# A two-block vision tower on one core: the first norm of the second block's tokens moved into rows of tokens, and routed slots counted with a running sum

## The chip, the cores and the metric

One NeuronCore of one Trainium2 chip. The metric is device time in microseconds (us) of one execution. Engines are named as in the profile: PE is TensorE (PEld its weight loads), DVE VectorE, ACT ScalarE, POOL GpSimd, SP SyncE.

## The reference, cut to what matters

128 images of 3 x 176 x 208 become 143 patches of 16 x 16 and a class token: 144 tokens (S) of 128 features (D) each. Block 0 adds a gated state-space layer and an FFN with 8 experts, of which each token takes 2. Block 1 adds windowed attention and an FFN with one expert of 16 per image. What the change touches is the end of block 0's FFN and the norm behind it:

```python
x = _ln(mv + x, ln2_g, ln2_b)                  # x2, 128 features a token
logits = x @ gate_w + gate_b
topv, topi = jax.lax.top_k(logits, 2)
probs = jax.nn.softmax(topv, axis=-1)          # the two weights
moe = sum over the two experts of weight * expert(x)
x = _ln(moe + x, ln3_g, ln3_b)                 # called norm 3 below
h = h + x                                      # h2 in the kernel
h = h + attention(_layernorm(h))               # that norm is norm 4 below
```

All in fp32.

## The kernel before, in words

The work goes in 32 items of 4 images (T = 576 tokens). Three stages follow each other. Activations lie feature by feature (128 partitions) x token, so a norm over features is a matmul with the matrix `center` (which takes the mean away), a Square, a matmul with `mean`, and a Ln and an Exp (for the root) on full tiles of 128 x 576.

**Stage A** (lines 496 to 1046) computes block 0 up to the router. It is a pipeline by hand: in each of 35 steps four items x, y, z, w at different depths pass through, and each engine has its own `step` function, whose order of jobs is fixed (PE 557, ACT 685, DVE 825, POOL 1018, SP 367). Engines wait for each other on semaphores. Item z is routed: `turn` (534) transposes x2 into rows of tokens, 96 partitions (G) x 6 groups (NG) x 128; ACT copies them out of PSUM as `rows` (741, 750); DVE finds the two best experts (`route_...`, 934 to 1009). The place of a token in its expert's list is a rank: the tokens that chose the expert before it. `ranks` (543) forms it on PE: one matmul of `before` (ones above the diagonal) over the 96 tokens of the group, five that add each group's picks to all later groups, and one for the tokens of former items (`chosen`). Each fp32 matmul runs as two passes. POOL scatters the rows into `expert_in` by 12 indirect DMAs; SP stores h1 and x2, both feature by token, to HBM. Five table loads of ACT stand in a step (688, 702, 734, 760, 775), the one at 688 at the very beginning, though 775 has loaded the same set at the end of the step before.

**Stage B** (1053 to 1294) runs 152 blocks of 256 rows through their experts.

**Stage C** (1297 to 1961) is again a pipeline by hand, of 36 steps; in step t it holds items v = t, w = t-1, x = t-2, y = t-3, z = t-4. PSUM has banks A0, A1 for projections and others for scores. For v: SP loads h1c and x2c; DVE writes row numbers (`place`, 1829); POOL gathers 12 x 96 rows of `expert_out` (1466), multiplies them by the weights (1474) and adds the two choices to `ysum` (1479); PE transposes `ysum` to features (`moe`, 1506, 6 transposes, at the end of the step, 1705). For w: DVE adds x2c (`prec`, 1885); PE centres it (1664), ACT squares (`square`, 1716), PE takes the mean (1674), ACT Ln and Exp (`inverse_root`, 1720), DVE multiplies (`x3`, 1937) and adds bias and h1c (`h2`, 1943). Norm 4 of h2 follows (1688, 1696, 1718 to 1724, `xq` 1961). For x: attention in nine units, each a round of scores (PE 1528), `minimum` (DVE 1842), `exps` (ACT 1747), `turn` (PE 1550, a transposition), `turned` (ACT 1756), `values` (PE 1558), and `halves` and `heads` (DVE 1848 to 1861, ends in `att`). Units 6 to 8 of an item are finished in the next step, when it is y; then its projection, `h` (1911), norm 5 (`xm`, 1923, from bank A1), `means` (1932) and the routing of the image. For z: gates (`gdiag`, 1990) and last layer. Each engine takes the jobs of all items in the order of its `step` (PE 1602, ACT 1763, DVE 1877), in which a late result holds up everything behind it.

## Time and profile before

| | us |
|---|---|
| median of 3 runs | 3320.6 (3319.63 to 3323.88) |
| the profiled execution | 3318.28 |
| its span, first to last instruction | 3316.4 |
| PE busy in the span | 2775.0 |
| DVE, ACT, POOL busy | 1901.2, 1843.2, 1134.6 |
| mean granted clock of PE | 0.901 of full |

How to read it: the profile is one execution of the program on the chip, seen by the hardware's profiler. Busy time is that of instructions at work; an engine that waits is idle. The start of a matmul is measured, its end is modelled. The rows below are from the trace of this execution; times count from the first instruction.

### The profile page before, as it was taken

How to read it: one execution, taken by the hardware profiler on the slowest of the kernel's cores; microseconds unless marked ns; L12 is line 12 of the kernel's file. 1: busy time of each engine (PE TensorE's matmuls, PEld its weight loads, DVE VectorE, ACT ScalarE, POOL GpSimd, SP SyncE). 2: the span in 40 equal slices, each digit the busy share in tenths (PEclk: the TensorE clock that was granted, in tenths of full speed). 3: DMA queues.
4: the chain of work that ended last, by engine and by line, in shares of the span. 5: the costliest groups of instructions: out<-in, count | busy, mean ns of one | idle time of the engine just before them, and what ended most of it. 6: DMA issues, size and time to landing. Idle time of an engine off the chain costs nothing.

```text
span 3316.4 us, 69976 instructions
## 1 busy us (share of the span) xinstructions
PE 2775.0 (84%) x25687; PEld 2181.5 (66%) x25687; DVE 1901.2 (57%) x4527; ACT 1843.2 (56%) x3725; POOL 1134.6 (34%) x964
## 2 busy tenths in 40 slices
PE   6999999999999859999996677877788777877787
PEld 4766666666666549999995456655566555655565
DVE  4878878878788742222221355655565555655566
ACT  4777777777777734444443345544454444544454
POOL 1454555655555530000002533333333333333310
PEclk9999999999999979999998688887888888878888
DMA  3222222222222137777774111111111111111110
GB/s 119 88 84 72 96 83 72 101 78 75 100 76 73 42 114 228 228 230 227 230 228 140 34 40 41 29 41 44 44 40 27 43 44 43 40 28 44 44 30 26
DMA packets 139758, 287.14 MB, mean 87 GB/s; under 512 B 25440, under 2 KB 82784, under 8 KB 135392
## 3 DMA queue, kind: packets, MB, share of 16 engines
q1 hardware_dynamic: 114912, 245.68, 22.9%
q0 software_dynamic: 24576, 37.80, 4.2%
q8 instruction: 177, 2.90, 0.4%
q14 instruction: 93, 0.76, 0.1%
HBM read 215.08 MB, written 68.29 MB: 85 GB/s over the span
## 4 chain that ended last, share of the span: by engine, by line
PE 47%; issue 7%; another core or an unknown queue 4%; DVE 3%; ACT 1%; POOL 1%; DMA 0%; SPq 0%; DVEq 0%; ACTq 0%; POOLq 0%
PE psum L1174 8%; PE psum L1165 8%; PE psum L1538 7%; PE psum L1498 5%; PE psum L1555 3%; PE psum L1568 3%; PE psum L1523 2%; PE psum L1503 2%; PE psum L1580 2%; DVE qdiag L1837 1%; PE psum L1598 1%; PE psum L1156 1%; PE psum L1546 1%; DVE inv L1852 1%
## 5 line engine op out<-in xcount | busy, mean ns | idle before, releaser
L1466 POOL DMA_INDIRECT ycho<-expert_out,place x384 | 367.5, 957 | 1417.4 <-DVE place L1829 1309.7
L1208 ACT ACTIVATE hid<-psum,w_blk 128x256 f32<-128x256 f32 x608 | 269.1, 474 | 326.2 <-PE psum L1165 326.2
L1039 POOL DMA_INDIRECT expert_in<-rows,slot_i x384 | 392.3, 1022 | 133.2 <-issue 111.6
L1852 DVE RECIPROCAL inv<-psum 128x64 f32<-128x64 f32 x288 | 159.5, 554 | 464.7 <-remote 385.9
L1538 PE MATMUL psum<-keys,qdiag 64*64 64x80 f32 x4608 | 281.4, 256 | 124.1 <-issue 123.7
L1752 ACT ACTIVATE ex<-psum,smin 128x80 f32<-128x80 f32 x1152 | 282.2, 332 | 142.9 <-DVE smin L1845 135.8
L1538 PEld LDWEIGHTS psum<-keys,qdiag 64*64 64x64 f32 x4608 | 214.8, 148 | 211.1 <-issue 195.7
L502 PE MATMUL psum<-xn,w_in 128*128 128x288 f32 x1024 | 311.1, 429 | 39.6 <-DVE xn L861 10.2
L1174 PE MATMUL psum<-w_blk,hid 128*128 128x128 f32 x2432 | 296.6, 275 | 0.0
L1568 PE MATMUL psum<-ex_t,pair_ones 128*32 128x64 f32 x4608 | 137.8, 244 | 189.6 <-DVE half L1853 124.0
L1165 PE MATMUL psum<-x_t,w_blk 128*128 128x256 f32 x1216 | 289.5, 381 | 2.4 <-DMA w_blk<-w_exp_in 2.4
L1174 PEld LDWEIGHTS psum<-w_blk,hid 128*128 128x128 f32 x2432 | 283.7, 192 | 0.1
L1760 ACT ACTIVATE ex_t<-psum 128x512 f32<-128x512 f32 x288 | 174.1, 605 | 174.6 <-PE psum L1555 92.2
L502 PEld LDWEIGHTS psum<-xn,w_in 128*128 128x128 f32 x1024 | 187.8, 196 | 111.4 <-DVE xn L861 23.5
L1015 POOL TENSOR_TENSOR unit<-unit 128x576 f32<-128x576 f32 x64 | 119.4, 1865 | 393.7 <-ACT unit L671 276.2
L1568 PEld LDWEIGHTS psum<-ex_t,pair_ones 128*32 128x32 f32 x4608 | 86.5, 119 | 240.8 <-DVE half L1853 128.5
L1165 PEld LDWEIGHTS psum<-x_t,w_blk 128*128 128x128 f32 x1216 | 212.8, 191 | 34.4 <-DMA w_blk<-w_exp_in 2.8
L1273 DVE COPY x_t<-psum 128x256 f32<-128x256 f32 x152 | 64.6, 425 | 230.5 <-PE psum L1156 230.5
L508 PE MATMUL psum<-xin,w_tok 128*128 128x286 f32 x768 | 194.0, 409 | 2.5 <-DVEq L469 2.5
L1555 PE MATMUL psum<-cst,ex 128*128 128x128 f32 x1152 | 182.0, 280 | 7.5 <-ACT ex L1752 5.2
L1281 DVE TENSOR_TENSOR rows_out<-psum,w_blk 128x256 f32<-128x256 f32 x152 | 64.6, 425 | 215.7 <-PE psum L1174 215.7
L805 DVE SCALAR_TENSOR_TENSOR acc<-pj,taps,acc 128x576 f32<-128x576 f32 x192 | 182.3, 950 | 0.1
(247 smaller groups left out, 5848.5 us busy)
## 6 DMA issues: line engine op xcount, KB each, us to landing
w_blk<-w_exp_in SPq DMA_DIRECT2D x152, 578.0 KB, 3.8
xin<-x_in SPq DMA_DIRECT2D x32, 1716.0 KB
rows_in<-expert_in SPq DMA_DIRECT2D x152, 128.0 KB, 2.3
expert_out<-rows_out SPq DMA_DIRECT2D x152, 128.0 KB, 3.0
h_dram<-h SPq DMA_DIRECT2D x32, 288.0 KB
x_dram<-x SPq DMA_DIRECT2D x32, 288.0 KB
h1c<-h_dram SPq DMA_DIRECT2D x32, 288.0 KB
x2c<-x_dram SPq DMA_DIRECT2D x32, 288.0 KB
```

Source lines behind the costliest of these rows:

```text
L502: last = nc.tensor.matmul(bank[:, g, 0:T2], w, two(src)[:, g, :], start=True, stop=True)
L508: last = nc.tensor.matmul(bank[:, g, 0:2 * NPATCH], w_tok[:, k, :], xin[x.s][:, k, g * 2 * NPATCH:(g + 1) * 2 * NPATCH], start=(k == 0), s ...
L1039: pool.indirect_dma_start(out=expert_in[:, :], out_offset=bass.IndirectOffsetOnAxis(ap=slot_i[z.s][:, n:n + 1], axis=0), in_=rows[z.s][:, ...
L1165: nc.tensor.matmul(HB[b.s][c % HK], w_blk[b.q][:, c * 128:(c + 1) * 128], x_t[b.s][:], start=True, stop=True).then_inc(hid_done[b.s], 1)
L1174: last = nc.tensor.matmul(YB[b.s][:, t * 128:(t + 1) * 128], hid[b.s][:, c, t * 128:(t + 1) * 128], w_blk[b.q][:, FF + c * D:FF + (c + 1) ...
L1208: nc.scalar.activation(hid[b.s][:, c, :], HB[b.s][c % HK], ACT.Gelu_apprx_tanh, bias=w_blk[b.q][:, FF + FC * D + c:FF + FC * D + c + 1]).t ...
L1466: pool.indirect_dma_start(out=ycho[x.s][:, k, :], out_offset=None, in_=expert_out[:, :], in_offset=bass.IndirectOffsetOnAxis(ap=place[x.s] ...
L1538: nc.tensor.matmul(bank[at, b * QK:(b + 1) * QK], qdiag[at, u * UB + b, :, :].rearrange("p j q -> p (j q)"), keys[at, m, key_range(qb)], s ...
L1555: done = nc.tensor.transpose(XB[0:KW, b * 128:(b + 1) * 128], ex[u][:, b, :], C("ident"))
L1568: nc.tensor.matmul(sum_bank()[at], pair_ones[:, j, :], ex_t[u % RING][:, :, t * PH + j * QB:t * PH + (j + 1) * QB], start=(j == 0), stop=( ...
L1752: done = nc.scalar.activation(ex[u][:, b, in_window(qb)], score_bank(u)[:, b * QK:(b + 1) * QK], ACT.Exp, bias=smin[u % RING][:, b:b + 1], ...
L1852: v.reciprocal(inv[:], sum_bank()).then_inc(head_step, 1)
```

## The change

Stage A. `before` has 1 taken from every entry, so that it also subtracts the group's own column sum. `picks` and a new tile `upto_g` lie expert by group on the free axis; `within` is 1 except at the first group of each expert, and one scan over 48 elements (`tensor_tensor_scan`) gives in `upto_g` the picks of this and all former groups. It takes the place of the reduction `newly`. The rank is then three matmuls in place of seven, and PE waits for the scan (step 15 of the routing) instead of `picks` (step 13). `chosen` takes its sum from `upto_g`. The table load at the beginning of a step (688) is gone; one is done before the first step. x2 is stored to HBM in rows of tokens, from `rows`, once ACT has copied them; DVE no longer waits for the store two items back, ACT does before it overwrites `rows`.

Stage B. Two constants more are made before the blocks: `shift3` (the centred ln3_b) by one matmul and a copy, and ln3_b is added to `att_bias`.

Stage C. Norm 3 is done in rows of tokens ahead of the transposes. x2c is loaded as rows (96 x 768); POOL adds it to the gathered rows in a third operation. DVE takes statistics of each token (6 `bn_stats`, 6 `bn_aggr`, in two places of its order), ACT the root (a Ln and an Exp of 96 x 6), DVE the product -mean x root (`move3`), ACT writes `nrows` = ysum x root + move3 in 6 instructions of 96 x 128. PE transposes `nrows`, now in the step of w, to bank A1 where `prec` was centred; DVE makes h2 = A1 x ln3_g + h1c in one operation from PSUM. ln3_b is left out of h2 and comes back as `shift3` in norm 4 (in the Square and in `xq`) and in `att_bias`. Gone are `prec`, the two projections of norm 3, its Square, Ln and Exp, and `x3`. POOL's last sum waits for `nrows` of the item before, where it waited for the transposes.

The diff, cut to its core (indentation cut by 8; declarations, constants and semaphores left out):

```diff
@@ -124,7 +124,7 @@
 "ident": np.eye(128),
-"before": (p[:, None] < p[None, :])[:, :G],
+"before": (p[:, None] < p[None, :])[:, :G] - 1.0,
 "ones": np.ones((128, 128)),
@@ -372,8 +379,9 @@
         if z:
-            hold(sp, x2_step, z.upto(2, 2))
-            sp.dma_start(x2_dram[:, a_range(z.n, z.s)], x2[z.s][:]).then_inc(x2_stored[z.s], 16)
+            hold(sp, rows_ready, z.upto(2, 2))
+            sp.dma_start(x2_dram[row_range(z.n, z.s), :], rows[z.s][:].rearrange("p g d -> p (g d)")
+                         ).then_inc(x2_stored[z.s], 16)
@@ -542,15 +553,12 @@
-        pe.wait_ge(route_step, z.upto(ROUTE, 13))
+        pe.wait_ge(route_step, z.upto(ROUTE, 15))
         if z.old(1):
...
         dst = rank_bank(bank)
-        nc.tensor.matmul(dst, C("before")[0:G, :], picks[z.s][:], start=True, stop=False)
-        for g in range(NG - 1):
-            nc.tensor.matmul(dst[:, g + 1:NG, :], C("ones")[0:G, 0:G],
-                             picks[z.s][:, g:g + 1, :].to_broadcast([G, NG - 1 - g, E]),
-                             start=False, stop=False)
+        nc.tensor.matmul(dst, C("before")[0:G, :], by_group(picks[z.s][:]), start=True, stop=False)
+        nc.tensor.matmul(dst, C("ones")[0:G, 0:G], by_group(upto_g[z.s][:]), start=False, stop=False)
         nc.tensor.matmul(dst, C("ones")[0:G, 0:G], chosen[:].unsqueeze(1).to_broadcast([G, NG, E]),
@@ -685,7 +694,6 @@
-        act.preload_act_table_set("gelu_apprx_tanh_and_others")
         if y:
@@ -738,6 +746,7 @@
                 act.wait_ge(scattered[z.s], 16 * 2 * NG * z.n)
+                act.wait_ge(x2_stored[z.s], 16 * z.n)
             nc.scalar.activation(rows[z.s][:, 0:4, :].rearrange("p g d -> p (g d)"), A0[0:G, 0, 0:4 * 128],
@@ -863,8 +872,6 @@
             v.wait_ge(rstd3, z.upto(1, 1))
-            if z.old(2):
-                v.wait_ge(x2_stored[z.s], 16 * z.n)
             v.scalar_tensor_tensor(out=two(x2[z.s][:]), in0=both(A1), scalar=shift1[:, 0:1], in1=two(rf[:]),
@@ -966,11 +973,10 @@
     route_after(v, z, 12)
-    v.tensor_tensor(picks[s][:], pick1[s][:], pick2[s][:], ALU.add).then_inc(route_step, 1)
+    v.tensor_tensor(by_group(picks[s][:]), pick1[s][:], pick2[s][:], ALU.add).then_inc(route_step, 1)
     v.tensor_tensor(wexp[s][:], top2[s][:], top1[s][:], ALU.subtract).then_inc(route_step, 1)
     route_after(v, z, 13)
-    v.tensor_reduce(newly[s][:], picks[s][:].rearrange("p g e -> p e g"), AX_X, ALU.add
-                    ).then_inc(route_step, 1)
+    v.tensor_tensor_scan(upto_g[s][:], within[:], picks[s][:], 0.0, ALU.mult, ALU.add).then_inc(route_step, 1)
@@ -978,7 +984,7 @@
         v.wait_ge(chosen_new, z.upto(1, 0))
-    v.tensor_tensor(chosen[:], chosen[:], newly[s][:], ALU.add).then_inc(chosen_new, 1)
+    v.tensor_tensor(chosen[:], chosen[:], by_group(upto_g[s][:])[:, NG - 1, :], ALU.add).then_inc(chosen_new, 1)
     v.tensor_tensor(cand[s][:], rank_bank(bank), R("first")[0:G, :].unsqueeze(1).to_broadcast([G, NG, E]),
@@ -1423,7 +1437,10 @@
         sp.dma_start(h1c[x.s][:], h1_dram[:, a_range(x.n, x.s)]).then_inc(h_landed[x.s], 16)
-        sp.dma_start(x2c[x.s][:], x2_dram[:, a_range(x.n, x.s)]).then_inc(h_landed[x.s], 16)
+        if x.old(2):
+            hold(sp, ysum_step, x.upto(YSUM, -YSUM))
+        sp.dma_start(x2c[x.s][:].rearrange("p g d -> p (g d)"), x2_dram[row_range(x.n, x.s), :]
+                     ).then_inc(x2_landed[x.s], 16)
@@ -1473,11 +1490,13 @@
                            ).then_inc(ysum_step, 1)
-        pool.wait_ge(ysum_step, x.upto(2, 1))
+        pool.wait_ge(x2_landed[x.s], 16 * x.n + 16)
+        pool.wait_ge(ysum_step, x.upto(YSUM, 1))
+        pool.tensor_tensor(x2c[x.s][:], x2c[x.s][:], ycho[x.s][:, 0:NG, :], ALU.add).then_inc(ysum_step, 1)
+        pool.wait_ge(ysum_step, x.upto(YSUM, 2))
         if x.old(1):
-            pool.wait_ge(moe_done, x.upto(1, 0))
-        pool.tensor_tensor(ysum[:], ycho[x.s][:, 0:NG, :], ycho[x.s][:, NG:, :], ALU.add
-                           ).then_inc(ysum_step, 1)
+            pool.wait_ge(nrows_ready, x.upto(1, 0))
+        pool.tensor_tensor(ysum[:], x2c[x.s][:], ycho[x.s][:, NG:, :], ALU.add).then_inc(ysum_step, 1)
@@ -1504,9 +1523,9 @@
     def moe(x, bank):
-        pe.wait_ge(ysum_step, x.upto(2, 2))
+        pe.wait_ge(nrows_ready, x.upto(1, 1))
         for g in range(NG):
-            last = nc.tensor.transpose(bank[:, g // 3, (g % 3) * G:(g % 3 + 1) * G], ysum[:, g, :],
+            last = nc.tensor.transpose(bank[:, g // 3, (g % 3) * G:(g % 3 + 1) * G], nrows[:, g, :],
                                        C("ident")[0:G, 0:G])
@@ -1660,25 +1677,15 @@
                 pe.wait_ge(val_ready, x.upto(NV, 2))
-            pe.wait_ge(prec_ready, w.upto(1, 1))
-            project(A1, C("center"), prec[:]).then_inc(norm3_pe, 1)
+            moe(w, A1)
         if x:
...
             values(x, 2)
-        if w:
-            if y:
-                pe.wait_ge(norm5_act, y.upto(3, 2))
-            elif x:
-                pe.wait_ge(k_ready, x.upto(1, 1))
-            pe.wait_ge(norm3_act, w.upto(3, 1))
-            project(A0, C("mean"), sq3[:]).then_inc(norm3_pe, 1)
         if x:
...
         if y:
-            if w:
-                pe.wait_ge(norm3_act, w.upto(3, 2))
             router(y, A0)
@@ -1692,17 +1699,13 @@
                 pe.wait_ge(pick_step, y.upto(PICK, 1))
+            elif x:
+                pe.wait_ge(k_ready, x.upto(1, 1))
             pe.wait_ge(norm4_act, w.upto(3, 1))
...
             turn(x, 6)
-        if v:
-            if w:
-                pe.wait_ge(norm4_act, w.upto(3, 2))
-            elif v.old(1):
-                pe.wait_ge(prec_ready, v.upto(1, 0))
-            moe(v, A0)
         if x:
@@ -1713,9 +1716,24 @@
-    def square(x, dst, bank, pe_done, done):
+    def square(x, dst, bank, pe_done, done, **bias):
         act.wait_ge(pe_done, x.upto(2, 1))
-        nc.scalar.activation(two(dst[:]), both(bank), ACT.Square).then_inc(done, 1)
+        nc.scalar.activation(two(dst[:]), both(bank), ACT.Square, **bias).then_inc(done, 1)
...
+    def row_root(x):
+        act.wait_ge(stats_ready, x.upto(1, 1))
+        nc.scalar.activation(root3[:], stats[:, :, 1], ACT.Ln, bias=eps_col[0:G, 0:1]).then_inc(root_step, 1)
+        act.wait_ge(root_step, x.upto(2, 1))
+        nc.scalar.activation(root3[:], root3[:], ACT.Exp, scale=-0.5).then_inc(root_step, 1)
...
+    def normed_rows(x):
+        act.wait_ge(moved_ready, x.upto(1, 1))
+        if x.old(1):
+            act.wait_ge(moe_done, x.upto(1, 0))
+        for g in range(NG):
+            last = nc.scalar.activation(nrows[:, g, :], ysum[:, g, :], ACT.Identity, bias=move3[:, g:g + 1],
+                                        scale=root3[:, g:g + 1])
+        last.then_inc(nrows_ready, 1)
@@ -1782,29 +1800,29 @@
             exps(x, 1)
+        if w:
+            row_root(w)
+        if x:
             turned(x, 0)
...
             exps(x, 2)
+        if w:
+            normed_rows(w)
         if y:
...
             exps(x, 3)
-        if w:
-            square(w, sq3, A1, norm3_pe, norm3_act)
         if x:
...
             turned(x, 3)
-        if w:
-            inverse_root(w, r3, A0, norm3_pe, norm3_act)
-        if x:
             exps(x, 5)
...
         if w:
-            square(w, sq4, A1, norm4_pe, norm4_act)
+            square(w, sq4, A1, norm4_pe, norm4_act, bias=shift3[:, 0:1])
         if x:
@@ -1859,6 +1877,28 @@
                         one_head[:], inv[:], ALU.mult).then_inc(att_ready, 1)
...
+    def row_halves(x):
...
+        v.wait_ge(ysum_step, x.upto(YSUM, YSUM))
+        for g in range(NG):
+            last = v.bn_stats(halves3[:, g, :], ysum[:, g, :])
+        last.then_inc(halves3_ready, 1)
...
+    def row_stats(x):
+        v.wait_ge(halves3_ready, x.upto(1, 1))
+        if x.old(1):
+            v.wait_ge(moved_ready, x.upto(1, 0))
+        for g in range(NG):
+            last = v.bn_aggr(stats[:, g, :], halves3[:, g, :])
+        last.then_inc(stats_ready, 1)
...
+    def row_moves(x):
+        v.wait_ge(root_step, x.upto(2, 2))
+        if x.old(1):
+            v.wait_ge(nrows_ready, x.upto(1, 0))
+        v.scalar_tensor_tensor(out=move3[:], in0=stats[:, :, 0], scalar=-1.0, in1=root3[:], op0=ALU.mult,
+                               op1=ALU.mult).then_inc(moved_ready, 1)
@@ -1898,9 +1934,13 @@
             pick_gate(v, z)
+        if w:
+            row_halves(w)
         if y:
...
             heads(y, 8)
+        if w:
+            row_stats(w)
         if x:
@@ -1912,6 +1952,8 @@
             minimum(x, 2)
+        if w:
+            row_moves(w)
         if z:
@@ -1933,16 +1975,12 @@
         if w:
-            v.wait_ge(norm3_act, w.upto(3, 3))
-            v.scalar_tensor_tensor(out=two(x3[:]), in0=both(A1), scalar=V("ln3_g"), in1=two(r3[:]),
-                                   op0=ALU.mult, op1=ALU.mult).then_inc(x3_ready, 1)
+            v.wait_ge(moe_done, w.upto(1, 1))
+            v.wait_ge(h_landed[w.s], 16 * w.n + 16)
+            v.scalar_tensor_tensor(out=two(h2[:, w.s * T:(w.s + 1) * T]), in0=both(A1), scalar=V("ln3_g"),
+                                   in1=two(h1c[w.s][:]), op0=ALU.mult, op1=ALU.add).then_inc(h2_ready, 1)
         if x:
             halves(x, 3)
-        if w:
-            v.wait_ge(x3_ready, w.upto(1, 1))
-            v.scalar_tensor_tensor(out=h2[:, w.s * T:(w.s + 1) * T], in0=x3[:], scalar=V("ln3_b"), in1=h1c[w.s][:],
-                                   op0=ALU.add, op1=ALU.add).then_inc(h2_ready, 1)
-        if x:
             heads(x, 3)
@@ -1958,8 +1996,8 @@
                 v.wait_ge(val_done, w.upto(NV, 0))
-            v.tensor_tensor(two_two(xq[:]), both(A1).rearrange("p g (m n) -> p g m n", m=2),
-                            two(r4[:]).rearrange("p g (m n) -> p g m n", m=2), ALU.mult).then_inc(xq_ready, 1)
+            v.scalar_tensor_tensor(out=two(xq[:].rearrange("p m n -> p (m n)")), in0=both(A1), scalar=shift3[:, 0:1],
+                                   in1=two(r4[:]), op0=ALU.add, op1=ALU.mult).then_inc(xq_ready, 1)
```

## Rows read from the trace of the kernel before

**Rows 1.** The page, first part: busy time, share of span, instructions.
```profile
PE 2775.0 (84%) x25687; PEld 2181.5 (66%) x25687; DVE 1901.2 (57%) x4527; ACT 1843.2 (56%) x3725; POOL 1134.6 (34%) x964
```

**Rows 2.** Stretches: length, busy us by engine, granted clock, DMA share, GB/s.
```profile
601.36:636.30 34.94, 31.86 (x148) 23.59 (x148) 28.48 (x57) 26.54 (x38) 19.72 (x16) 1.00 0.25 85
...
2450.00:2478.00 28.00, 28.00 (x445) 21.78 (x442) 20.91 (x59) 18.01 (x52) 3.49 (x2) 0.90 0.03 7
2432.00:2450.00 18.00, 6.68 (x90) 4.90 (x91) 4.53 (x14) 3.62 (x9) 12.58 (x13) 0.68 0.31 88
3221.00:3257.00 36.00, 35.58 (x606) 27.64 (x605) 27.75 (x81) 25.65 (x71) 0.00 (x0) 1.00 0.11 32
```

**Rows 3.** Timeline, stage A: start, length, engine, work, count [idle before <-releaser].
```profile
605.39 0.24 DVE L972 TENSOR_REDUCE newly<-picks 96x8 f32<-96x48 f32 x1
...
605.46 0.34 PE L549 MATMUL psum<-picks,cst 96*96 96x48 f32 x2 [1.40 <-ACT unit L671]
...
605.63 0.98 PE L551 MATMUL psum<-picks,cst 96*96 96x40 f32 x10
...
606.65 1.20 PE L502 MATMUL psum<-xn,w_in 128*128 128x288 f32 x4
...
608.86 0.74 ACT L772 ACTIVATE rf<-psum,eps_col 128x576 f32<-128x576 f32 x1 [1.15 <-PE psum L502]
...
609.75 6.02 PE L508 MATMUL psum<-xin,w_tok 128*128 128x286 f32 x24
...
612.39 1.28 ACT L688 ACT_TABLE_LOAD   x1
...
616.77 0.74 ACT L682 ACTIVATE view<-psum,mv_bias 128x576 f32<-128x576 f32 x1 [2.34 <-PE psum L502]
```

**Rows 4.** Timeline of PE in one step of stage C.
```profile
2465.10 1.19 PE L1498 MATMUL psum<-prec,cst 128*128 128x288 f32 x4
2466.12 0.60 PE L1555 MATMUL psum<-cst,ex 128*128 128x128 f32 x4
...
2467.24 1.24 PE L1498 MATMUL psum<-sq,cst 128*128 128x288 f32 x4
2468.41 0.77 PE L1538 MATMUL psum<-keys,qdiag 64*64 64x80 f32 x16
...
2472.30 1.19 PE L1503 MATMUL psum<-h,cst 128*128 128x288 f32 x4
```

**Rows 5.** Timeline of ACT and DVE in the same step.
```profile
2457.75 0.82 DVE L1911 SCALAR_TENSOR_TENSOR h<-psum,att_bias,h 128x576 f32<-128x576 f32 x1 [1.73 <-PE psum L1498]
...
2461.16 0.99 ACT L1752 ACTIVATE ex<-psum,smin 128x80 f32<-128x80 f32 x4
...
2462.32 0.74 ACT L1722 ACTIVATE r<-psum,eps_col 128x576 f32<-128x576 f32 x1 [0.17 <-PE psum L1498]
...
2463.81 0.76 DVE L1923 TENSOR_TENSOR xm<-psum,r 128x576 f32<-128x576 f32 x1
...
2464.91 0.98 ACT L1752 ACTIVATE ex<-psum,smin 128x80 f32<-128x80 f32 x4
...
2468.61 0.75 DVE L1932 TENSOR_REDUCE means<-xm 128x4 f32<-128x576 f32 x1
```

**Rows 6.** Groups by shape: count | busy us, mean ns | idle us before.
```profile
L1752 ACT ACTIVATE ex<-psum,smin 128x80 f32<-128x80 f32 x1152 | 282.2, 332 | 142.9 <-DVE smin L1845 135.8 <-issue 5.1
...
L816 DVE TENSOR_TENSOR_SCAN unit<-decays,unit 128x576 f32<-128x576 f32 x64 | 86.1, 1345 | 0.0
...
L1479 POOL TENSOR_TENSOR ysum<-ycho 96x768 f32<-96x768 f32 x32 | 57.9, 1808 | 2.5
...
L1990 DVE TENSOR_SCALAR gdiag<-cst,g 4x4 f32<-4x4 f32 x32 | 38.0, 1188 | 1.1
...
L768 ACT ACTIVATE wsum<-wexp,cst 96x6 f32<-96x6 f32 x32 | 9.6, 300 | 1.0
...
L766 ACT ACTIVATE wexp<-wexp 96x6 f32<-96x6 f32 x32 | 6.2, 192 | 1.0 <-DVE wexp L970 1.0
```

More of the change, by code:

```diff
@@ L223, in build @@
         consts_ready = sem("consts_ready")
-        held = {"sync": sem("held_sync"), "pool": sem("held_pool"), "tensor": sem("held_tensor")}
+        held = {"sync": sem("held_sync"), "pool": sem("held_pool"), "tensor": sem("held_tensor"),
+                "vector": sem("held_vector")}
         def first(n):
@@ L276, in build @@
         logit, lmask, cand = pair("logit", [G, NG, E]), pair("lmask", [G, NG, E]), pair("cand", [G, NG, E])
-        pick1, pick2, picks = pair("pick1", [G, NG, E]), pair("pick2", [G, NG, E]), pair("picks", [G, NG, E])
+        pick1, pick2, picks = pair("pick1", [G, NG, E]), pair("pick2", [G, NG, E]), pair("picks", [G, E * NG])
         top1, top2, best = pair("top1", [G, NG]), pair("top2", [G, NG]), pair("best", [G, NG])
         wexp, wsum = pair("wexp", [G, NG]), pair("wsum", [G, NG])
-        newly = pair("newly", [G, E])
+        upto_g, within = pair("upto_g", [G, E * NG]), sb("within", [G, E * NG], F32, mem_a)
         slot = pair("slot", [G, 2 * NG])
@@ L320, in rank_bank, with by_group @@
             return bank[0:G, 1, 0:NG * E].rearrange("p (g e) -> p g e", e=E)
+        def by_group(ap):
+            return ap.rearrange("p (e g) -> p g e", g=NG)
         def pairs(ap):
@@ L326, in a_range, with row_range @@
             return bass.DynSlice((2 * i + s) * T, T)
+        def row_range(i, s):
+            return bass.DynSlice((2 * i + s) * G, G)
         LAST = 2 * ITERS - 1
@@ L400, in a_prep_vector @@
             step(v.memset(chosen[:], 0.0))
+            step(v.memset(within[:], 1.0))
+            settle()
+            step(v.memset(by_group(within[:])[:, 0, :], 0.0))
             for s in range(2):
@@ L666, in a_scalar @@
             act.wait_ge(consts_ready, 4)
+            act.preload_act_table_set("gelu_apprx_tanh_and_others")
             def unit_out(x, u, bank):
@@ L1187, in b_tensor @@
             pe.wait_ge(loaded_c, 16 * 3)
-            nc.tensor.matmul(TB[1][:, 0:1], w_att[:], V("v_b"), start=True, stop=True).then_inc(bias_done, 1)
+            nc.tensor.matmul(TB[1][:, 0:1], w_att[:], V("v_b"), start=True, stop=True)
+            nc.tensor.matmul(TB[1][:, 1:2], C("center"), V("ln3_b"), start=True, stop=True).then_inc(bias_done, 1)
             pe.wait_ge(table_ready, 1)
@@ L1250, in b_vector @@
             v.wait_ge(bias_done, 1)
-            v.tensor_tensor(att_bias[:], TB[1][:, 0:1], V("attn_b"), ALU.add).then_inc(c_ready, 1)
+            chain(v.tensor_tensor(att_bias[:], TB[1][:, 0:1], V("attn_b"), ALU.add))
+            v.tensor_tensor(att_bias[:], att_bias[:], V("ln3_b"), ALU.add)
+            v.tensor_copy(shift3[:], TB[1][:, 1:2]).then_inc(c_ready, 1)
             v.tensor_copy(band[:], C("band"))
@@ L1310, in ring_c @@
             return [sb(f"{name}{k}", shape, dt, mem_c) for k in range(RING)]
-        h1c, x2c = pair_c("h1c", [128, T]), pair_c("x2c", [128, T])
+        h1c, x2c = pair_c("h1c", [128, T]), pair_c("x2c", [G, NG, D])
         ycho, ysum = pair_c("ycho", [G, 2 * NG, D]), one_c("ysum", [G, NG, D])
-        prec, x3 = one_c("prec", [128, T]), one_c("x3", [128, T])
-        sq3, r3, sq4, r4, sq5, r5 = (one_c(name, [128, T]) for name in ("sq3", "r3", "sq4", "r4", "sq5", "r5"))
+        halves3, stats = one_c("halves3", [G, NG, 6]), one_c("stats", [G, NG, 2])
+        root3, move3, nrows = one_c("root3", [G, NG]), one_c("move3", [G, NG]), one_c("nrows", [G, NG, D])
+        sq4, r4, sq5, r5 = (one_c(name, [128, T]) for name in ("sq4", "r4", "sq5", "r5"))
         h2, h3, xm = one_c("h2", [128, 2 * T]), one_c("h3", [128, 2 * T]), one_c("xm", [128, T])
@@ L1346, in build @@
         PICK = 9
+        YSUM = 3
         C_LAG = 4
@@ L1463, in gather @@
                 if x.old(2):
-                    hold(pool, moe_done, x.upto(1, -1))
+                    hold(pool, ysum_step, x.upto(YSUM, -YSUM))
                 for k in range(2 * NG):
@@ L1881, in step @@
                     row_numbers(v_)
-                if w:
-                    v.wait_ge(moe_done, w.upto(1, 1))
-                    v.wait_ge(h_landed[w.s], 32 * w.n + 32)
-                    v.tensor_tensor(two(prec[:]), both(A0), two(x2c[w.s][:]), ALU.add).then_inc(prec_ready, 1)
                 if y:
```

13 lines of the change are left out of this document (7 added, 6 removed).

## The prediction, made before the changed kernel was run

> **What bounds the kernel now.** I read the page first: TensorE (PE) is busy 84% of the span, VectorE (DVE) 57%, ScalarE (ACT) 56%, GpSimd (POOL) 34% [rows 1]. That is a mean over three stages, so I went on to stretches. One step of stage A, of 32, lasts 34.94 us with PE busy 31.86, DVE 28.48 and ACT 26.54 [rows 2]. Stage B (the experts) is not touched, except for one small matmul and three small DVE operations ahead of it. A step of stage C has two parts: 18 us in which PE works 6.68 at a granted clock of 0.68 while POOL gathers, and 28 us in which PE is busy all 28.0, DVE 20.9, ACT 18.0 and POOL 3.5. A step near the end, with no gather, takes 36 us in all [rows 2]. So C loses some 10 us a step to the gather's part, whose cause the trace doesn't name, and has a full PE in the rest. A full PE does not say that PE alone is the limit: in C the engines run one order written by hand, and what counts is how long before its use each result stands ready. For that I followed one step of each stage on the timeline.
>
> **Stage A, ranks.** PE starts the first of seven matmuls (14 passes) at 605.46, after 1.40 us of idle that ACT ends, and the next job at 606.65. The last twelve passes take 606.65 - 605.63 = 1.02 us, 0.085 each. Three matmuls are left, six passes, 0.51. But PE now waits for the scan, which stands where the reduction `newly` ends at 605.63 [rows 3]. A scan of 48 elements is not in the trace; the one of 576 takes 1.345 us [rows 6], so between 0.11 (in proportion) and 0.24 (like the reduction, which is nearest in size and which I take). PE starts some 0.25 us late and gains 1.19 - 0.51 - 0.25 = 0.43; bounds 0 and 0.68. Does it pass on? Behind the ranks stand unit 5 and the variance; ACT's logarithm waits 1.15 us for PE at 608.86, and the embedding at 609.75 waits for that logarithm [rows 3]; both move up. I take 0.4 x 32 = 13 us.
>
> **The table load** of a step's beginning (1.28 us) falls out of ACT while PE embeds for 6.02 us, and ACT then idles 2.34 us for PE before the first view [rows 3]: 0 on the path. Without that cover it would be 1.28 x 32 = 41 us. **The x2 store** is one DMA as before, behind `rows` instead of `x2`. On SP only the next step's load stands behind it, which waits for that step's embedding anyway. DVE loses a wait and ACT gets one, on a store two steps old: 0. The operations ahead of stage B hide behind the last scatter: 0; uncovered they would be under 1 us, once.
>
> **Stage C, removed.** PE: two projections, one from 2465.10 to the next job at 2466.12 (1.02 us), one from 2467.24 to 2468.41 (1.17) [rows 4]; the six transposes (some 0.5 us) move from a step's end to the place of the first. ACT: Square, Ln and Exp of 576 columns, some 2.1 us. DVE: `prec` and `x3`, some 1.5 us. **Added.** POOL: a sum of 768 columns, 1.81 us [rows 6], behind the gather, where POOL is idle 24.5 of 28 us [rows 2]; with that cover gone, 1.81 a step. `ysum` is one buffer, so POOL's last sum now waits for the rows of the item before, until the middle of the step, near 2464.5; behind it on POOL stands only the next gather, 13 us later. SP's load of x2c gets a wait for a sum two steps old: 0. DVE: six statistics of 128 columns and six merges of six numbers. A reduction of 48 inputs takes 0.24 [rows 3], one of 576 0.75 [rows 5]; 128 gives 0.32, less some overlap, 1.4 to 1.9 for six; the merges 0.1 to 0.2 each. That is 2.0 to 3.1 us ahead of `h`, before which DVE idles 1.73 [rows 5]; I take 2.3. The 0.6 that is left hides behind the last layer, which PE does meanwhile. ACT: a Ln and an Exp of six columns, some 0.5 us, in idle time, and six Identity of 128 columns.
>
> **The price of those six decides.** An Exp of 96x6 takes 0.192 us, an Identity of that size whose bias is read per partition 0.300: a pointer costs 0.108. An exp of 80 columns with one pointer takes 0.332 [rows 6], four together 0.99, so they overlap by 0.113; a Ln of 576 with one pointer takes 0.74 [rows 5], so a column costs 0.82 ns. One of 128 columns with one pointer is then 0.371, with two (scale and bias) 0.48; six are 5 x 0.367 + 0.48 = 2.3 us. Lower bound, as if with one pointer: 1.7; upper, with no overlap: 2.9. The Trainium skill (ScalarE: Activation LUTs, What ACT_TABLE_LOAD costs) states 186 ns, 0.833 ns a column and 93 ns for each pointer, with 93 of overlap; by it the six cost an estimated 2.4 us, and the sum would be some 3 us higher. The trace agrees as to the pointer, with 108 ns.
>
> **Where they stand.** They follow the exps that end at 2462.15. Ln(y) had 0.17 us of idle before it and now starts near 2464.5; so `xm` moves from 2463.81 to 2465.95, and the exps of 2464.91 to 2466.35 [rows 5]. PE comes to the transposes at 2465.1, but they need bank A1, which `xm` reads until 2466.7: 1.6 us of idle where PE worked before. They take 0.5; then turn 3 (was 2466.12) waits for the exps until 2467.4, values for a head of DVE until 2467.95, and the scores that stood at 2468.41 start near 2468.55. The 1.7 us that PE lost by then (1.02 + 1.17 - 0.5) are eaten. DVE lags too: `means` (was 2468.61) ends near 2470.65, the minimum after it 2471.1, its exps 2472.1, and scores of PE wait for these. Centring h2 (was 2472.30 [rows 4]) starts near 2472.95, 0.65 us late. Some 0.5 of this would be lost even if the rows cost nothing, since the mean's projection covered the heads of DVE. At a step's end Ln, Exp and `xq` follow PE's last mean, over 2.2 us by their lengths [rows 5], longer than what PE has left to do without the transposes: their going buys nothing. Thirty steps hold all three items: 30 x 0.65 = 19.5 us. Once, in the fill, rows cost 1.8 (POOL's sum) and some 0.7 more.
>
> **Sum**, against the profiled execution of 3318.3 us (span 3316.4): 3318.3 - 13 + 19.5 + 2.5 = 3327.3. The median of the three runs is 2.3 higher, so 3329.6, told as 3330.
>
> **Rivals.**
> 1. *PE is the limit and the rows are absorbed.* For: PE busy 28 of 28, ACT only 18 [rows 2]. A step then gains 1.7 less the 0.5 of uncovered heads, 1.2: 3320.6 - 13 + 2.5 - 36 = 3274. Against: the exps end at 2465.89 and turn 3 starts at 2466.12, 0.23 us of slack [rows 4, 5]. Chance 0.19.
> 2. *C evens out*, the six Identity near their lower bound: 3320.6 - 13 + 2.5 = 3310, give or take 7. Chance 0.20.
> 3. *POOL's last sum stands in DVE's way.* It now falls among the heads of x, from 2464.5 to 2466.3. gdiag, an operation of 4x4, takes 1.19 us on average beside POOL's sums [rows 6]; if an `att` or `xm` meets this sum and is held like that, the late DVE is later by 1 us: 30 more, 3360. By my times the `att` next to it stand at 2462.3 and 2467.9; it decides once one of them shifts by 1.6 us. The Trainium skill (SBUF — State Buffer, SBUF: two separate sides) calls the pair of ports that both engines share an exclusive lock, which holds off a DVE operation with two inputs in SBUF beside a POOL one: an `att` would be held, `xm`, whose one input is in PSUM, would not. Chance 0.10.
> 4. *Stage A gives nothing*, being DVE's chain (28.5 of 34.9 busy): 3330 + 13 = 3343. Chance 0.08.
> 5. *The change does not do what it says*: the gather's part shifts by what the rest gives, and nothing can be told, 3321. Chance 0.05.
>
> **Numbers.** The forecast has 0.38, with a range of its own of 3322 to 3346. A measurement of this kernel can tell about 0.2% from no change, 6.6 us. Slower by more: 0.30 of the forecast, rivals 3 and 4: 0.48. Within: 0.08 of the forecast, 0.07 of rival 2, rival 5: 0.20. Faster: rival 1, 0.13 of rival 2: 0.32. The range runs from rival 1 to rival 3, 3272 to 3360.
>
> **What would show it.** Six Identity in 2.3 us; PE idle for over 1 us before the transposes, ended by `xm`; a part of C outside the gather near 28.6 us; steps of A of 34.5 us with ranks in 0.5. It would be wrong if steps of C fell below 45 us, if the transposes did not wait, if a statistic took over 0.35 us, or if the gather's part were other than some 18 us.

## The result, and the profile after

Slower, by a little over half a per cent: 3336.99 us (3332.2 to 3350.56, five runs) against 3321.97 (3319.63 to 3323.88, five runs), ratio 1.0055, 95% interval 1.0043 to 1.0068. The profiled execution took 3333.95 us, 15.7 more than the one of before, and its span is 3332.1. In two later sets of runs the same kernel stood at 1.0057 [1.0045, 1.0069] and 1.0056 [1.0043, 1.0069].

First the page's busy times, which answer to [rows 1]:

```profile
PE 2715.4 (81%) x25177; PEld 2119.2 (64%) x25177; DVE 1910.6 (57%) x4883; ACT 1810.4 (54%) x3853; POOL 1194.3 (36%) x996
```

PE has 60 us less to do and ACT 33 us less, and yet the kernel is longer: the work taken away was not what set the end. Where the time went is read from one line of each kernel that occurs once a step. First of before, then of after (count: least, median, most ns, first and last start in us, shapes):

```profile
L969 DVE TENSOR_TENSOR picks<-pick x32: 190/193/203, 111.5 to 1190.4; 96x48 f32<-96x48 f32 x32
L1961 DVE TENSOR_TENSOR xq<-psum,r x32: 757/758/759, 1836.0 to 3252.7; 128x576 f32<-128x576 f32 x32
```

```profile
L976 DVE TENSOR_TENSOR picks<-pick x32: 225/230/244, 112.7 to 1186.2; 96x48 f32<-96x48 f32 x32
L1999 DVE SCALAR_TENSOR_TENSOR xq<-psum,shift,r x32: 816/818/818, 1829.0 to 3268.5; 128x576 f32<-128x576 f32 x32
```

Stage A's 31 steps take 1073.5 us for 1078.9, 5.4 less. Stage C's 31 take 1439.5 for 1416.7, 22.8 more, 0.73 a step. The fill of stage C, from the first row numbers (1796.5, now 1791.1) to the first `xq`, takes 37.9 us for 39.5. Stage A starts 1.2 us later and stage B is 1.2 us shorter, which cancels. The sum, -5.4 + 22.8 - 1.6 = 15.8, is then the difference of the spans, 15.7 by their rounded values.

**The new work**, in groups by shape (busy us, mean ns | idle before):

```profile
L1734 ACT ACTIVATE nrows<-ysum,move,root 96x128 f32<-96x128 f32 x192 | 77.4, 498 | 0.2 <-issue 0.2
...
L1499 POOL TENSOR_TENSOR ysum<-x2c,ycho 96x768 f32<-96x768 f32 x32 | 57.8, 1806 | 319.6 <-ACT nrows L1734 319.4
L1885 DVE BATCH_NORM_STATS2 halves<-ysum 96x6 f32<-96x128 f32 x192 | 39.7, 267 | 23.5 <-POOL ysum L1499 23.5
...
L1528 PE MATMUL psum<-cst,nrows 96*128 96x96 f32 x192 | 23.3, 259 | 76.4 <-DVE xm L1965 40.2 <-ACT nrows L1734 36.1
...
L1893 DVE BATCH_NORM_AGGREGATE stats<-halves 96x2 f32<-96x6 f32 x192 | 16.0, 149 | 0.1
...
L979 DVE TENSOR_TENSOR_SCAN upto_g<-within,picks 96x48 f32<-96x48 f32 x32 | 8.1, 254 | 0.0
```

Ahead of the transposes PE now idles 40.2 us for `xm`; the 36.1 for `nrows` are one wait, in the fill. The same step as in [rows 4, 5], on the timeline (start, length, ..., [idle <-releaser]), ACT, DVE and PE:

```profile
2461.91 0.98 ACT L1770 ACTIVATE ex<-psum,smin 128x80 f32<-128x80 f32 x4
2462.75 2.42 ACT L1734 ACTIVATE nrows<-ysum,move,root 96x128 f32<-96x128 f32 x6
2465.06 0.73 ACT L1740 ACTIVATE r<-psum,eps_col 128x576 f32<-128x576 f32 x1
...
2466.54 0.76 DVE L1965 TENSOR_TENSOR xm<-psum,r 128x576 f32<-128x576 f32 x1 [2.05 <-ACT r L1742]
...
2467.35 0.71 PE L1528 MATMUL psum<-cst,nrows 96*128 96x96 f32 x6 [1.34 <-DVE xm L1965]
...
2473.59 1.19 PE L1522 MATMUL psum<-h,cst 128*128 128x288 f32 x4
```

The six rows stand between the exps and the logarithm as forecast; the logarithm waits for nothing but them.

**What the mean of a step hides.** Steps of stage C come in up to three lengths, by how long PE is granted 1.2 GHz (granted clock 0.50 in the rows) and not 2.4 (1.00). One step of after cut at the clock's changes, then one long step (length, busy us of PE, PEld, DVE, ACT, POOL, granted clock):

```profile
2432.62:2440.50 7.88, 4.90 (x56) 3.76 (x56) 3.47 (x11) 3.29 (x9) 5.27 (x6) 1.00 0.55 155
2440.50:2454.30 13.80, 6.44 (x82) 5.07 (x82) 4.17 (x11) 2.35 (x8) 10.23 (x9) 0.51 0.13 29
2454.30:2479.18 24.88, 22.25 (x404) 16.70 (x388) 18.44 (x63) 16.87 (x51) 2.36 (x2) 1.00 0.03 8
2572.68:2621.55 48.87, 36.43 (x522) 27.50 (x522) 25.98 (x85) 22.64 (x67) 17.83 (x15) 0.79 0.14 37
```

And two steps of before:

```profile
1969.89:2015.13 45.24, 34.75 (x538) 26.41 (x530) 25.87 (x74) 22.12 (x61) 16.07 (x14) 0.85 0.15 41
2291.25:2339.31 48.06, 37.21 (x538) 28.43 (x530) 25.95 (x73) 22.12 (x61) 16.07 (x14) 0.79 0.14 38
```

The clock falls after PE has idled in the gather's part of the step: in the first of these steps PE's matmuls are over at 2437.7, and the low stretch begins at 2440.5. A mean of 0.85 over 45.24 us means 2 x 0.15 x 45.24 = 13.6 us at the lower level; 0.79 over 48.06 means 20.2. Sorted in this way, 27 steps of each trace in full flow (steps from row numbers to row numbers, mean lengths):

| us at 1.2 GHz | before | after |
|---|---|---|
| 14 | 13 steps, 45.66 us | 22 steps, 46.67 us |
| 17 | 9 steps, 46.41 | none |
| 20 to 21 | 5 steps, 48.06 | 5 steps, 48.81 |

At the same clock the changed step costs 1.0 us more where the low stretch is short and 0.75 where it is long. The mean over the 27 is 0.72, because before had the middle kind in 9 steps. The short steps of before themselves spread from 45.24 to 46.49 us, those of after only from 46.54 to 46.92.

### The profile page after: what moved, and what is told of

It reads as the page before. It is cut to its first block, busy times and chain, and to the rows that moved or that the text cites. A ratio compares the mean times of both kernels' runs of the same rounds, so it can differ in the third digit from the quotient of the medians.

```text
span 3332.1 us, 69506 instructions
## 1 busy us (share of the span) xinstructions
PE 2715.4 (81%) x25177; PEld 2119.2 (64%) x25177; DVE 1910.6 (57%) x4883; ACT 1810.4 (54%) x3853; POOL 1194.3 (36%) x996
## 4 chain that ended last, share of the span: by engine, by line
PE 35%; DVE 8%; ACT 7%; issue 7%; another core or an unknown queue 6%; POOL 1%; DMA 0%; SPq 0%; DVEq 0%; ACTq 0%; POOLq 0%
PE psum L1180 8%; PE psum L1171 8%; PE psum L1557 4%; PE psum L1517 2%; ACT nrows L1734 2%; ACT ex L1770 2%; PE psum L1574 2%; PE psum L1522 2%; PE psum L1587 2%; DVE inv L1870 2%; PE psum L1542 1%; ACT r L1740 1%; ACT r L1742 1%; DVE qdiag L1855 1%
## 5 line engine op out<-in xcount | busy, mean ns | idle before, releaser
L1557 PE MATMUL psum<-keys,qdiag 64*64 64x80 f32 x4608 | 295.4, 257 | 141.7 <-issue 134.0
L1557 PEld LDWEIGHTS psum<-keys,qdiag 64*64 64x64 f32 x4608 | 223.0, 148 | 228.6 <-issue 186.7
```

Of the source, the lines that this page charges most:

```text
L1557: nc.tensor.matmul(bank[at, b * QK:(b + 1) * QK], qdiag[at, u * UB + b, :, :].rearrange("p j q -> p (j q)"), keys[at, m, key_range(qb)], s ...
```

## The experiments

Twelve runs on three chips. On chips X and Z the kernel before took 3321.24 and 3320.08 us; on Y it took 3341.32, with a mean granted clock of 0.886 to 0.890 where X and Z show some 0.900. So a ratio from Y is not set against one from X or Z. The changed kernel itself was not run on Y; what stands for it there is e2_table_back, called its twin below.

The two repeats answer one question. One story on record was that the ratio would wander between 0.995 and 1.006 with the number of long steps, its rival that it is the code's and would come again within 0.0015. It came again on X and on Z, within 0.0002 of the first, although the traced execution on X had 11 long steps of 27 and that on Z 4. Both stories allow that value; the closeness speaks for the code, as far as chips like X and Z go.

| run | chip | us | ratio to before, 95% interval |
|---|---|---|---|
| after_again | X | 3339.05 | 1.0057 [1.0045, 1.0069] |
| after_third | Z | 3339.86 | 1.0056 [1.0043, 1.0069] |
| e1_ranks_only | Y | 3336.8 | 0.9983 [0.9974, 0.9992] |
| e2_table_back | Y | 3329.45 | 0.9961 [0.9949, 0.9973] |
| e2_table_again | Z | 3343.36 | 1.0074 [1.0062, 1.0086] |
| a2_ranks_twice | X | 3349.12 | 1.0087 [1.0072, 1.0102] |
| e3_rows_early | Y | 3293.1 | 0.985 [0.9837, 0.9863] |
| e3_rows_again | Z | 3310.18 | 0.9972 [0.9959, 0.9984] |
| e4_nrows_after_root | Y | 3353.49 | 1.0033 [1.0022, 1.0044] |
| g1_half_gather | X | 3110.26 | 0.936 [0.9346, 0.9373] |
| g2_gather_later | X | 3291.9 | 0.9922 [0.9908, 0.9937] |
| g3_rows_in_gather | Z | 3291.08 | 0.9922 [0.9897, 0.9947] |

**The ranks of stage A alone, put into the kernel before** (the table load and the store of x2 stay as before).

```diff
-nc.tensor.matmul(dst, C("before")..., picks...)       # and five more, group by group
+nc.tensor.matmul(dst, C("before")[0:G, :], by_group(picks[z.s][:]), start=True, stop=False)
+nc.tensor.matmul(dst, C("ones")[0:G, 0:G], by_group(upto_g[z.s][:]), start=False, stop=False)
...
-v.tensor_reduce(newly[s][:], ...)
+v.tensor_tensor_scan(upto_g[s][:], within[:], picks[s][:], 0.0, ALU.mult, ALU.add)
```

> The kernel before with one part of the change alone: in the first block the picks are written expert by expert and the ranks come from the running sum and three products; the table load, the store of x2 and the whole second block are as before. Theory (the gain reaches the embedding and is lost again in VectorE's chain behind it; the two traces give -0.15 us per step of the first block, -5.4 us at its end): 3316.6 us against 3322, between -3 and -8. Rival, my forecast's term (-0.4 us per step, 32 steps): -13, 3309. Rival, the first block's gain came from the table load or the store and not from the ranks: 3322, within 2 us. Rival, the ranks' gain is reached only with the rest: slower than before by up to 3 us, because the scan writes across a stride.

0.9983 is -5.7 us of 3341, as the theory had it; the forecast's -13 lies outside the interval (-3 to -9). Its stage A takes 1070.5 us, that of the twin on the same chip 1072.5: what the twin has besides, the store of x2 behind the copied rows, gained nothing that shows.

**PE's work on the ranks made longer again.**

```diff
+for _ in range(4):
+    nc.tensor.matmul(dst, C("before")[0:G, :], by_group(picks[z.s][:]), start=True, stop=True)
 nc.tensor.matmul(dst, C("before")[0:G, :], by_group(picks[z.s][:]), start=True, stop=False)
```

> The changed kernel with TensorE's work on the ranks in the first block put back in length: four more products of the picks ahead of the right one, about +0.35 us per step. Theory (0.35 us of the ranks were worth 0.15 us of a step): +3 to +7 us, ratio to the changed kernel 1.001 to 1.002. Rival (TensorE is the limit of the first block's step): +0.35 to 0.4 us per step, +11 to +13 us, ratio 1.0035 to 1.004. Rival (the ranks are hidden altogether, the first block gained by something else): within 1 us.

It cost 10 us against after_again on the same chip, with an extra 0.7 us of ranks a step (eight passes more; 0.35 was expected), and stage A alone is 1086.4 us against 1076.3. How it costs is seen in two neighbouring steps of it, the second of the usual kind, and then in two of after (columns as above):

```profile
642.63:678.59 35.96, 33.16 (x148) 24.64 (x148) 28.69 (x58) 25.13 (x37) 18.94 (x16) 0.95 0.25 82
678.59:713.44 34.85, 31.72 (x148) 23.61 (x148) 28.51 (x59) 25.13 (x37) 19.42 (x16) 1.00 0.26 85
```

```profile
637.06:672.38 35.32, 32.53 (x140) 23.96 (x140) 28.69 (x58) 25.13 (x37) 18.94 (x16) 0.95 0.25 84
672.38:707.24 34.86, 31.43 (x140) 22.75 (x140) 28.50 (x58) 25.12 (x37) 20.03 (x16) 1.00 0.26 85
```

A step of stage A in which the clock stays up lasts 34.9 us whatever the ranks take, in all three kernels. A step in which it falls for some 3.4 us (mean 0.95) can be longer. Of 29 steps, before has 12 with such a fall, 9 of them longer, at 35.64 us; after has 12 too, only 4 of them longer, at 35.33; here there are 14 (one with 6.8 us) and all are longer, at 35.92. So the number of falls is much the same, and the length of the ranks shows in how many of these steps are drawn out, and by how much. That accounts for nearly all of the differences of stage A; that the fall is what lets the ranks through is read from the traces, no run varies it. None of the three stories told on record had this, and the 10 us lie between the first's 3 to 7 and the second's 11 to 13.

**The table load put back.**

```diff
 def step(x, y, z, w):
+    act.preload_act_table_set("gelu_apprx_tanh_and_others")
     if y:
         unit_out(y, 6, B1)
```

> The changed kernel with the load of the activation table put back at the head of each step of the first block, where the kernel before has it. Theory (it lies behind the embedding, where ScalarE waits for TensorE longer than the load takes): the same as the changed kernel within 2 us, 3337. Rival, it stands in ScalarE's chain: 32 x 1.28 = +41 us, 3378. In between, if the load sits on the step's critical instructions only in part: 3340 to 3350.

> The changed kernel with the table load put back, once more, now beside the changed kernel itself on one chip. On the first chip the kernel before had a mean granted clock of 0.888 and took 3341 us, so its ratio of 0.9961 can't be set against a ratio taken on another chip. Theory (the load is hidden): the changed kernel's own time within 3 us, ratio to the kernel before 1.0057 within 0.001. Rival (ScalarE's load helps, since what follows it starts later): 0.5 to 1% faster than the changed kernel.

On Z the load costs 3.5 us by the medians (3343.36 against 3339.86), with intervals that overlap; +41 is excluded. Its stage A takes 1072.8 us, that of after_third 1072.5, so the load is hidden as forecast; the traced executions differ in stage C, where this one has 13 long steps and that one 4. The run on Y has another use: this twin, the changed kernel but for a hidden load, is there faster than before, 0.9961. No trace of before was taken on Y, but e1's, whose stage C is that of before, has 21 of 27 steps of the 20 us kind, such as this one, where the twin has 5:

```profile
2052.08:2099.89 47.81, 37.77 (x539) 28.59 (x530) 26.21 (x74) 22.09 (x61) 16.07 (x14) 0.79 0.14 39
```

**The rows moved into the gather's part of the step.**

```diff
 # ScalarE
     exps(y, 8)
+    row_root(w); normed_rows(w)      # taken from behind exps(x, 1) and exps(x, 2)
     key(x, A0)
 # VectorE
     queries(x)
+    row_halves(w); row_stats(w); row_moves(w)
```

> The changed kernel with the work on the rows of tokens moved into the stretch in which both engines wait for the gather of the next tile: VectorE takes halves, stats and move behind the queries' stripes, ScalarE takes root and the six normed rows ahead of the keys. Theory (the second block's step is longer because the six Identity stand ahead of the inverse root of the third norm and push xm and the transposes back by 2.1 us, and because VectorE has 1.9 us more in the busy stretch; in the idle stretch of 7 us on ScalarE and 6 us on VectorE both are free): per step xm 2.1 us earlier, TensorE's idle of 1.3 us ahead of the transposes gone, centre of h2 1.2 to 1.9 us earlier, a step of 44.5 to 45.2 us for 46.4; 31 steps give -37 to -59 us against the changed kernel: 3278 to 3300, faster than both kernels. Rival 1 (TensorE is the limit of that stretch once xm is back where it was, as in the kernel before): a step of 45.7, 3314. Rival 2 (while the indirect transfers of the gather run, ScalarE's and VectorE's results come late as TensorE's do, so the keys and qdiag are pushed back instead): the step stays at 46.4 or grows, 3337 to 3350.

> The changed kernel with the rows' work moved ahead of the keys, once more beside the changed kernel on one chip. Theory (45.0 to 45.2 us for a step in place of 46.4 to 46.9, both from traces): 37 to 50 us faster than the changed kernel, 3287 to 3302, ratio to the kernel before 0.990 to 0.994. Rival (the ratio of 0.985 measured on the first chip holds on every chip): 3272.

On Z 29.7 us faster than after_third and 0.28% faster than before, on Y 1.5% faster than before. ACT on the timeline of e3_rows_early, then PE of the same step:

```profile
2062.52 2.42 ACT L1734 ACTIVATE nrows<-ysum,move,root 96x128 f32<-96x128 f32 x6 [0.23 <-issue]
2072.11 0.74 ACT L1755 ACTIVATE keys<-psum,col 128x576 f32<-128x576 f32 x1 [7.17 <-remote]
```

```profile
2088.99 0.22 PE L1567 MATMUL psum<-band,ident_h 128*128 128x128 bf16 x1
2089.04 0.67 PE L1528 MATMUL psum<-cst,nrows 96*128 96x96 f32 x6
```

The rows fit into idle time and PE reaches the transposes without a wait. From the step's start, `xm` comes at 32.15 us for 34.44, and the last matmul that centres h2 at 40.75 for 42.28, means over 26 steps. A step with the short low stretch takes 45.2 us on Y and 45.5 on Z, where the changed kernel takes 46.6 on both; that is also 0.1 to 0.4 less than in the trace of before. That is the test of the mechanism: the 1.0 us of the change is the rows' place, not their work. What it doesn't separate is ACT's rows from DVE's statistics and product, since the edit moves both. The size was less than expected on Z (30 us, not 37 to 50); in that trace 14 of 27 steps are of the 17 us kind, 46.8 us long.

**The rows behind the inverse root.**

```diff
-if w: normed_rows(w)
 if y: inverse_root(y, r5, A0, norm5_pe, norm5_act)
+if w: normed_rows(w)
```

> The changed kernel with one pair swapped in ScalarE's order: the six normed rows stand behind the inverse root of the third norm and not ahead of it. Theory (what costs is that the root, and so xm, waits for 2.4 us of rows): xm 2.1 us earlier, the transposes then wait for the rows and start about 0.9 us earlier than in the changed kernel, means earlier by 1 to 2; a step of 45.4 to 46.0 us for 46.4, -12 to -31 us: 3306 to 3325. Rival (the transposes and what follows them wait for ScalarE's sum of work and not for xm, since the next transposed exponentials come behind both): same as the changed kernel within 5 us, 3332 to 3342.

Neither held: on Y it is slower than before, 3353.49 us for 3341.32, while the twin is faster there, 3329.45. `xm` is early, but turned 2 and the exps now queue behind the rows, and PE waits twice:

```profile
2044.21 0.69 PE L1528 MATMUL psum<-cst,nrows 96*128 96x96 f32 x6 [0.97 <-ACT nrows L1734]
2045.54 0.63 PE L1574 MATMUL psum<-cst,ex 128*128 128x128 f32 x4 [0.65 <-ACT ex L1770]
```

And then the clock falls a second time in the step (stretch of the same trace):

```profile
2046.40:2049.20 2.80, 2.80 (x67) 2.23 (x61) 1.94 (x6) 0.46 (x1) 0.00 (x0) 0.50 0.03 6
```

All 27 steps have it, 17 us at 1.2 GHz in all (13.7 and 3.4) and 47.79 us long, 1.2 more than the short steps of the twin. The two short waits of PE, 1.6 us together, come right before this second fall and the cost goes with both; the runs don't separate them.

**Half of the gather** (the transfers of the second expert's rows are left out, and with them its share of the output).

```diff
-for k in range(2 * NG):
+for k in range(NG):
     pool.indirect_dma_start(out=ycho[x.s][:, k, :], ...)
```

> The changed kernel with six of the twelve indirect transfers of each tile left out: the rows of the second pick are zeros, so the output lacks the second expert's share. Theory (while the gather's transfers run TensorE's results reach the other engines 6 to 9 us late, twice in a row, and a step without a gather takes 32 to 36 us for 46.5): the stretch of late results is half as long, a step of 41 to 43 us, 31 steps: -105 to -170 us, 3167 to 3232. Rival (the delay comes from the large loads of h1c and x2c and the store of the output at the head of the step, or from the clock's fall): a step of 46 to 46.5, 3320 to 3337.

More than the theory had: 3110.26 us, 229 less than after_again, 7.4 us a step. One step of it:

```profile
2019.56:2059.57 40.01, 31.82 (x522) 24.51 (x522) 26.86 (x84) 22.35 (x67) 12.35 (x9) 0.91 0.14 38
```

POOL issues a transfer every 1.23 us, so six take 7.4. The usual step is 40.0 us for 46.7 of after_again's short ones, 6.7 less, and the rest is that after_again had 11 long steps and this trace none. So nearly all the time in which the six are issued is gained. The stretch at 1.2 GHz falls with it, from 13.7 to 6.8 us in the usual step, and the data moved in the gather is halved too: what of the gain is issue, transfer or clock isn't separated.

**The gather later in the step.**

```diff
-if v_: row_numbers(v_)        # at the step's head
 ...
 if x: minimum(x, 0)
+if v_: row_numbers(v_)
```

> The changed kernel with the rows' numbers, and so the gather of the next tile, issued behind the first minimum of the scores, some 10 to 20 us into the step, instead of at its head. Theory (the late results follow the gather): the first minimum comes at 10 to 12 us of the step for 20.3, and the stretch behind it is as much longer; the step's length within 3 us of 46.5, 3240 to 3430. Rival (the late results belong to the head of the step: its loads, its chain over the last tile's heads): the first minimum stays at 20 us, and the step is the same, 3332 to 3342.

The late results follow the gather: the first minimum comes 6.8 us behind the last step's `xq` for 20.2. On DVE and ACT of this kernel, 14 and 18 us behind the row numbers at 2013.32:

```profile
2027.28 0.82 DVE L1951 SCALAR_TENSOR_TENSOR h<-psum,att_bias,h 128x576 f32<-128x576 f32 x1 [10.34 <-remote]
```

```profile
2031.59 0.60 ACT L1778 ACTIVATE ex_t<-psum 128x512 f32<-128x512 f32 x1 [13.23 <-remote]
```

In the step's head `inv` and the keys no longer wait. As an extra that the theory's range allowed but did not forecast, the kernel is 47 us faster than after_again and 0.8% faster than before; steps with the short stretch take 44.2 to 45.5 us, 44.9 on average.

**Both moves together.** On top of the later gather, `normed_rows(w)` right behind `row_root(w)`, and `row_moves(w)` ahead of `h`.

> The changed kernel with both moves: the gather of the next tile behind the first minimum of the scores, and in the 10 to 13 us in which VectorE and ScalarE then wait for TensorE's late results, the move of the rows (VectorE, ahead of h3) and the six normed rows (ScalarE, right behind the rows' root). Theory (the six Identity cost 2.1 us ahead of xm, wherever the gather stands): xm about 2 us earlier than with the later gather alone, a step of 43 to 43.8 us for 44.7 to 45.2; 31 steps give -30 to -60 us against that kernel, 3232 to 3262, the fastest of all. Rival (the two savings are the same one, a stretch behind the gather that then waits for TensorE): 3285 to 3295, as with the later gather alone.

The rival won: 0.9922 (on Z), the ratio of the later gather alone (on X). The rows lie in idle time, but the result for which DVE waits comes later in turn, so that `h` stands at 17.17 us of the step for 12.81 and `xm` at 25.13 for 24.65:

```profile
2115.61 0.16 DVE L1899 SCALAR_TENSOR_TENSOR move<-stats,root 96x6 f32<-96x6 f32 x1 [1.45 <-issue]
2127.24 0.82 DVE L1952 SCALAR_TENSOR_TENSOR h<-psum,att_bias,h 128x576 f32<-128x576 f32 x1 [11.47 <-remote]
```

## Why the prediction was right, and what was off in it

The number (3330 for 3337), the sign and the mechanism in stage C hold. By its steps:

- *Six Identity, 2.3 us, bounds 1.7 to 2.9.* Measured 2.42, 498 ns each for 480. By the figures of the Trainium skill (ScalarE: Activation LUTs, What ACT_TABLE_LOAD costs) 2.4 had been estimated, which is nearer; the trace agrees with it. Right.
- *`xm` from 2463.81 to 2465.95.* Over 26 steps `xm` comes 2.1 us later into the step (34.44 for 32.34). Right.
- *1.6 us of PE's idle ahead of the transposes, ended by `xm`.* 40.2 us in 30 waits, 1.34 each. Right. The six transposes behind it take 0.7 us for the 0.5 of the estimate.
- *Centring h2 0.65 late, 30 x 0.65 = 19.5.* Its last matmul starts at 42.28 for 41.62, 0.66, and it is 22.8 in all for 31 steps. The gather's part of the step stands, as forecast: `h` comes at 26.35 us for 26.19. The size is right, but as a mean over steps at different clocks. The prediction's steps had one clock; at equal clock the loss is 1.0 us. Its working from one step met the mean by luck as well as by reasoning.
- *Statistics and merges, 2.3 us.* 1.24 and 0.50 for six of each. The statistic of 128 took 0.267 where its nearest rows gave 0.32, and the merges overlap; the 0.6 us that were to hide did not arise.
- *Stage A, 0.4 x 32 = 13 us.* This is the term that was mis-sized: -5.4. The ranks start 0.32 us later and their last matmul 0.35 earlier (6.13 us behind the logits for 6.48), and the embedding starts 0.29 earlier; that part is near the forecast. "I take 0.4 x 32" then took it as passed on by every step. Steps of 34.9 us don't pass it on, as a2_ranks_twice shows with 0.7 us in the other direction; only those in which the clock falls can. The sign "steps of A of 34.5 us" did not show, though the ranks took the 0.5 us. What fills 34.9 us isn't shown; rival 4 laid it to DVE's chain, which no run tests. Its result for stage A was nearer than its chance of 0.08.
- *The fill, +2.5.* Measured -1.6. The rows' work once is hidden in it.
- *The table load and the x2 store, 0.* With and without the load the two stages A on Z differ by 0.3 us, and e1 without the new store is not slower than the twin. Right.
- *Rival 1, PE the limit.* PE has 60 us less and nothing came of it in the changed kernel. But with the rows in idle time the kernel is faster than before on both chips (0.9972 and 0.985), so some of that gain was there to be had: e3_rows_again at 3310 is the number of rival 2, by another way.
- *Rival 3, POOL's sum in DVE's way.* The sum runs from 2465.31 to 2467.11, over `xm`, which takes 0.76 as before [rows 5]; so it is in 29 steps, with 0.757 us each, and no `att` meets the last sum. POOL's product does hold DVE, in both kernels: of 288 `att` in after, the 29 that start beside it take 0.76 us on average, the others 0.23.

```profile
2452.20 0.78 DVE L1878 TENSOR_TENSOR att<-one_head,inv 128x64 f32<-128x64 f32 x1
2463.02 0.22 DVE L1878 TENSOR_TENSOR att<-one_head,inv 128x64 f32<-128x64 f32 x1
```

The Trainium skill (SBUF — State Buffer, SBUF: two separate sides) has a DVE operation with two inputs in SBUF held beside one of POOL and one with an input in PSUM not; `xm` and `att` agree.

The sum: 3318.3 - 5.4 + 22.8 - 1.6 = 3334.1 is the profiled 3333.95. The forecast's 3327.3 was 6.7 low: 7.6 from stage A, 3.3 from stage C and -4.1 from the fill. That two of the misses partly cancel is luck.

## What to carry to other kernels

Work moved to an engine with idle time costs by where it stands in that engine's order. Here 2.4 us on ACT ahead of a result on which PE's next bank hangs, with 1.7 us on DVE, cost 1.0 us a step; the same work in a stretch in which both wait anyway cost nothing that shows. That version beats both kernels on chip Z, and on chip Y before and the changed kernel's twin; the later gather is better still, 0.8% under before. Before two versions within a per cent are judged, sort their steps by the granted clock: 14 of the 27 steps of before have a longer stretch at 1.2 GHz and are 0.7 to 2.4 us longer than the others. The ratio 1.0056 came again on X and Z, and yet on chip Y the twin came out ahead of before.
